# Feeding the experts of a mixture layer from a DRAM table instead of selection matmuls: 160 slots, a 32-row second tile in four column groups, four weight buffers

## The chip, the cores and the metric

One core of one Trainium2 chip runs the whole program. The metric is the device time in microseconds of one execution, as a median of several runs. One more execution was taken by the hardware profiler; all rows below come from that one.

## What is computed

One layer on 512 latent tokens of width 512 and a context of 8192 tokens, all in float32. In the reference:

```
x = x + cross_attention(layernorm(x), ctx)          # 16 heads, keys and values from 8192 context rows
x = x + self_attention(layernorm(x))                # softmax over a batch of one: value and output projections only
n = layernorm(x)
top_w, top_idx = top_k(n @ W_gate, 2); top_w = softmax(top_w)
for e in range(8):
    h = gelu(n @ W_in[e] + b_in[e])                 # 512 -> 2048
    y = h @ W_out[e] + b_out[e]                     # 2048 -> 512
    x = x + combine[:, e, None] * y                 # combine is zero for tokens that did not choose e
```

The reference computes every expert for every token; the kernel computes an expert only for the tokens that chose it (512 tokens, two choices, eight experts: 128 tokens an expert on average). With the seeded inputs the reference's gate gives the experts 113, 129, 159, 130, 134, 128, 92 and 139 tokens.

## The kernel before, in words

The change touches only the expert layer, the last 430 us of the span. Before it come the cross attention over the context, and `self_attention` (L770), in which SP already loads the first expert weights (`load_first`, L1025). `route` (L858) normalises x, computes the gate, the mask of the two choices, each token's rank within its expert (`r.rank`), the combine weights, and the flag `r.long`, which is set when an expert has more than SLOTS = 192 tokens.

`run_experts` (L1032) then walks over eight experts. Expert e has a column for each slot: 128 slots of a first tile, and 64 of a second tile that stand twice, so 256 columns. `select` (L1270) makes a 0/1 matrix of 512 tokens by 256 columns on VectorE; `gather` (L1149) multiplies the normalised tokens with it on TensorE, once for the high part and once for the low part, so that the tokens of the expert stand as columns. All large products are made of three fp32r products (high by high, high by low, low by high), which is why ScalarE rounds each weight tile to a high part (L1226, L1247) and VectorE subtracts to get the low part (L1267, L1306).

An expert is cut into four chunks (mc) of 512 hidden units. `hidden` (L1114) makes 4 x 3 x 4 = 48 matmuls of 256 columns for a chunk; ScalarE applies gelu; `output` (L1130) makes 12 fp32r matmuls of 512 columns for the first tile and, for the second tile, four plain fp32 matmuls in two column groups of 64 (L1144; each is two instructions in the trace, so 8). `turn_sel` (L1162) transposes the selection with 8 matmuls, and `scatter` (L1170) multiplies the expert's result (split again in high and low) with it, 16 matmuls of 512 columns an expert, which VectorE adds to x_sb (`add`, L1280).

The order on TensorE is written out by hand in `expert` (L1191): hidden 0, half of the scatter of the expert before, hidden 1, the other half, output 0, turn_sel, hidden 2, output 1, hidden 3, half of the gather for the next expert, output 2, the other half, output 3. Each engine has its own such list, and semaphores tie them. SP loads weights of 1 MB a transfer into two buffers of each kind, and waits for the low split or for `y_done` before it refills one. After the last expert four stores of 256 KB write x_sb to the output. A second call of `run_experts` (up to two more rounds of slots) stands behind the flag `r.long` and is skipped where no expert overflows.

Of the kernel before, what the change touches and what calls it, by code (L numbers as in the profile page):

```python
# [50 lines left out]
NX = 8  # L51
# [7 lines left out]
ROUNDS = -(-NQ // SLOTS)  # L59
# [710 lines left out]
def self_attention(nc, ctx, wv, bv, wo, bo, ident, x_sb, prefetch):  # L770
# [19 lines left out]

    with nc.Block() as block:
        @block.sync
        def _(sp):
            prefetch(sp)

# [62 lines left out]
def route(nc, ctx, w_gate, b_out, ident, x_sb, r):  # L858
# [6 lines left out]
    xn = sb("ro_xn", [P, QT, E])  # L865
# [16 lines left out]
    first = sb("ro_first", [P, QT, NX])  # L882
    second = sb("ro_second", [P, QT, NX])
# [12 lines left out]
    with nc.Block() as block:  # L896
# [6 lines left out]
        def _(pool):  # L903
# [3 lines left out]
            rounds = r.numbers[:, :].rearrange("p (r n) -> p r n", n=COLS)  # L907
            nc.gpsimd.iota(rounds[:, :, 0:P], pattern=[[SLOTS, ROUNDS], [1, P]], base=0, channel_multiplier=0,
                           allow_small_or_imprecise_dtypes=True).then_inc(made, 1)
            for copy in range(2):  # L910
                pool.wait_ge(made, copy + 1)
                nc.gpsimd.iota(rounds[:, :, P + copy * PAIRED:P + (copy + 1) * PAIRED], pattern=[[SLOTS, ROUNDS], [1, PAIRED]],
                               base=P, channel_multiplier=0, allow_small_or_imprecise_dtypes=True).then_inc(made, 1)
            pool.wait_ge(made, 3)
            nc.gpsimd.memset(every[:, :], 1.0).then_inc(made, 1)
            pool.wait_ge(made, 4)
            nc.gpsimd.affine_select(out=before[:, :], in_=every[:, :], compare_op=ALU.is_gt, fill=0.0,
                                    base=0, pattern=[[1, P]], channel_multiplier=-1).then_inc(made, 1)

        @block.tensor  # L920
        def _(pe):
# [8 lines left out]
            pe.wait_ge(made, 5)  # L930
# [25 lines left out]
        def _(dve):  # L956
# [29 lines left out]
            for t in range(QT):  # L986
                nc.vector.tensor_scalar(second[:, t, :], second[:, t, :], weight[:, 1, t:t + 1], None, ALU.mult).then_inc(link, 1)
            dve.wait_ge(masked, 1)
            dve.wait_ge(link, 5 + 5 * QT)
            for t in range(QT):  # L990
                nc.vector.scalar_tensor_tensor(r.combine[:, t, :], first[:, t, :], weight[:, 0, t:t + 1], second[:, t, :],
                                               ALU.mult, ALU.add).then_inc(link, 1)
# [6 lines left out]
            nc.vector.tensor_scalar(r.long[:, :], longest[:, :], float(SLOTS), None, ALU.is_gt).then_inc(done, 1)  # L999


class ExpertInputs:


    def __init__(self, nc, ctx):
        sb = lambda n, s: ctx.enter_context(nc.sbuf_tensor(n, s, F32))
        self.b_hidden = sb("ei_b_hidden", [P, NX, M // P])
        self.wi = [sb(f"ei_wi{b}", [P, ET, MC]) for b in range(2)]
        self.wo = [sb(f"ei_wo{b}", [P, MT, E]) for b in range(2)]

    def name_semaphores(self, nc, ctx, first_round):
        sem = lambda n: ctx.enter_context(nc.semaphore(f"ei{first_round}_{n}"))
        self.biases = sem("biases")
        self.wi_loaded = [sem(f"wi_loaded{b}") for b in range(2)]
        self.wo_loaded = [sem(f"wo_loaded{b}") for b in range(2)]

    def load_in(self, sp, w_in, e, mc):
        sp.dma_start(self.wi[mc % 2][:, :, :], w_in[bass.ds(e * E, E), mc * MC:(mc + 1) * MC]
                     .rearrange("(t p) m -> p t m", p=P)).then_inc(self.wi_loaded[mc % 2], 16)

    def load_out(self, sp, w_out, e, mc):
        sp.dma_start(self.wo[mc % 2][:, :, :], w_out[bass.ds(e * M + mc * MC, MC), :]
                     .rearrange("(t p) f -> p t f", p=P)).then_inc(self.wo_loaded[mc % 2], 16)

    def load_first(self, sp, w_in, b_in, w_out):  # L1025
        sp.dma_start(self.b_hidden[:, :, :], b_in).then_inc(self.biases, 16)
        for mc in range(2):
            self.load_in(sp, w_in, 0, mc)
            self.load_out(sp, w_out, 0, mc)


def run_experts(nc, ctx, rounds, w_in, b_in, w_out, ident, x_sb, out_dram, r, inputs):  # L1032
# [12 lines left out]
    expert_of = lambda step: step if STEPS == NX else step % NX  # L1045
# [6 lines left out]
    h = [sb(f"h{b}", [P, MT, COLS]) for b in range(2)]  # L1052
# [12 lines left out]
    bias_banks = [yp[:, t, :] for t in range(2)] + [hp[1][:, 2 * t:2 * t + 2, :].rearrange("p a n -> p (a n)") for t in range(2)]  # L1065
    move_g = move[:, :, :].rearrange("p a (b n) -> p (a b) n", n=COLS)
    b_ready, biased = map(sem, ("b_ready", "biased"))
# [7 lines left out]
    def guarded(eng, program):  # L1075

        if rounds[0] == 0:
            program()
        else:
            flag = eng.value_load(r.long[:, :], min_val=0, max_val=1)  # L1080
            with eng.If(flag > 0):
                program()

    with nc.Block() as block:
        @block.sync
        def _(sp):
# [11 lines left out]
            def program():  # L1098
                if rounds[0] > 0:
                    inputs.load_first(sp, w_in, b_in, w_out)  # L1100
# [4 lines left out]
                if rounds[0] > 0:  # L1105
                    sp.wait_ge(r.stored, 2 * 16 * QT)

            if rounds[0] > 0:
                sp.wait_ge(r.stored, 16 * QT)
# [3 lines left out]
        def _(pe):  # L1113
            def hidden(e, mc):  # L1114
# [4 lines left out]
                if rounds[0] == 0 and isinstance(n, int) and n == 1:  # L1119
                    pe.wait_ge(x_stands, QT)  # L1120
# [63 lines left out]
            def output_biases():  # L1184

                for t in range(QT):
                    last = nc.tensor.matmul(bias_banks[t], r.combine_t[:, t * P:(t + 1) * P], r.bo[:, :],  # L1187
                                            start=True, stop=True)
                last.then_inc(biased, 1)

# [20 lines left out]
            def program():  # L1211
                gather(0, 0)
                if rounds[0] == 0:
                    output_biases()
# [49 lines left out]
        def _(dve):  # L1264
# [5 lines left out]
            def select(e):  # L1270
                x = bass.ds(expert_of(e), 1)
                if STEPS == NX:
                    numbers = r.numbers[:, 0:COLS]
                else:
                    numbers = r.numbers[:, bass.ds((rounds[0] + e // NX) * COLS, COLS)]
# [177 lines left out]
```

## Time and profile before

| | |
|---|---|
| median of 3 runs | 1511.66 us (1506.25 to 1512.45) |
| span of the profiled execution, first to last instruction | 1510.6 us |
| start of the expert layer's first selection on VectorE | 1081.88 us |
| first hidden matmul | 1095.93 us |
| end of the last output matmul | 1494.9 us |
| expert layer's own stretch | 1081.9 to 1510.6 us |

The profile gives the span, not what lies around it; the span is 1.1 us under the median. A line of a group in the profile reads: line of the source, engine, operation, output tile, input tiles, shape, count; busy time in all and mean ns of one; idle time before them and who ended it. PE is the matrix engine, PEld its weight loads, DVE the VectorE, ACT the ScalarE, POOL the GpSimd. Matmuls overlap, so a mean duration is a latency; the spacing of matmuls is the length of a piece of the chain divided by its count.

### The profile page before, as it was taken

How to read it: one execution, taken by the hardware profiler on the slowest of the kernel's cores; microseconds unless marked ns; L12 is line 12 of the kernel's file. 1: busy time of each engine (PE TensorE's matmuls, PEld its weight loads, DVE VectorE, ACT ScalarE, POOL GpSimd, SP SyncE). 2: the span in 40 equal slices, each digit the busy share in tenths (PEclk: the TensorE clock that was granted, in tenths of full speed). 3: DMA queues.
4: the chain of work that ended last, by engine and by line, in shares of the span. 5: the costliest groups of instructions: out<-in, count | busy, mean ns of one | idle time of the engine just before them, and what ended most of it. 6: DMA issues, size and time to landing. Idle time of an engine off the chain costs nothing. (4 is left out here: it accounts for less than half of the span.)

```text
span 1510.6 us, 21218 instructions
## 1 busy us (share of the span) xinstructions
PE 1444.6 (96%) x7952; PEld 910.1 (60%) x7952; DVE 966.9 (64%) x846; ACT 811.0 (54%) x865; POOL 25.9 (2%) x24
## 2 busy tenths in 40 slices
PE   6999999999799999999999999977799999999996
PEld 4888888888433333333333333325688878887884
DVE  7444444443588888888888888865355556555653
ACT  4122122121488888888888888832264445444551
POOL 2000000000300000000000000000000000000000
PEclk9999999999899999999999999998599999999999
DMA  6855455454685555555555555203044544454441
GB/s 199 253 174 207 176 187 201 167 201 161 189 213 115 112 111 111 111 115 118 116 117 116 112 111 111 56 5 110 28 140 156 178 166 164 153 183 163 163 147 57
DMA packets 136180, 214.26 MB, mean 142 GB/s; under 512 B 7624, under 2 KB 40520, under 8 KB 136144
## 3 DMA queue, kind: packets, MB, share of 16 engines
q1 hardware_dynamic: 136144, 213.78, 48.9%
q8 instruction: 23, 0.38, 0.1%
q14 instruction: 13, 0.11, 0.0%
HBM read 159.23 MB, written 51.38 MB: 139 GB/s over the span
## 5 line engine op out<-in xcount | busy, mean ns | idle before, releaser
L659 ACT ACTIVATE at_p<-at_s 128x1024 f32<-128x1024 f32 x512 | 496.8, 1023 | 91.2 <-PE at_s L612 91.0
L679 DVE TENSOR_TENSOR p_sum<-p_sum,at_p 128x2048 f32 (+1 forms) x208 | 476.8, 2292 | 58.4 <-ACT at_p L659 50.9
L612 PEld LDWEIGHTS at_s<-q_stack,at_k 97*128 97x128 f32 x1024 | 172.8, 189 | 249.0 <-ACT at_p L659 162.2
L612 PE MATMUL at_s<-q_stack,at_k 97*128 (+1 forms) x1024 | 311.5, 424 | 7.7 <-PEq L440 7.0
L625 PE MATMUL at_o<-at_p,at_v 128*32 128x512 f32 x2048 | 273.0, 605 | 0.1
L409 ACT ACTIVATE sc_k_hi<-sc_kp,sc_bk 128x512 fp32r<-128x512 f32 x64 | 44.2, 691 | 125.8 <-PE sc_kp L377 125.8
L139 ACT ACTIVATE sc_c_hi<-sc_c 128x2048 fp32r<-128x2048 f32 x16 | 30.7, 1918 | 150.6 <-PE sc_vp L384 137.6
L1267 DVE TENSOR_TENSOR ex_wi_lo<-ei_wi,ex_wi_hi 128x2048 fp32r<-128x2048 f32 x32 | 73.3, 2289 | 51.2 <-ACT ex_wi_hi L1226 51.2
L341 DVE SCALAR_TENSOR_TENSOR sc_k_lo<-sc_kp,sc_bk,sc_k_hi 128x512 fp32r<-128x512 f32 x64 | 48.0, 750 | 89.3 <-ACT sc_k_hi L409 89.2
L349 DVE TENSOR_TENSOR sc_v<-sc_vp,sc_bv 128x512 f32<-128x512 f32 x64 | 44.1, 690 | 88.8 <-PE sc_vp L384 88.8
L1244 ACT ACTIVATE ex_h<-ex_hp,ex_b_cur 128x256 f32<-128x256 f32 x128 | 53.7, 471 | 86.7 <-PE ex_hp L1125 86.2
L625 PEld LDWEIGHTS at_o<-at_p,at_v 128*32 128x32 f32 x2048 | 40.3, 108 | 93.9 <-issue 92.9
L1306 DVE TENSOR_TENSOR ex_wo_lo<-ei_wo,ex_wo_hi 128x2048 fp32r<-128x2048 f32 x32 | 73.3, 2292 | 21.5 <-ACT ex_wo_hi L1247 21.5
L1125 PE MATMUL ex_hp<-ex_xg_hi,ex_wi_hi 128*128 128x256 f32 x512 | 85.3, 289 | 1.2 <-ACT ex_xg_lo L1231 1.2
L1125 PE MATMUL ex_hp<-ex_xg_hi,ex_wi_lo 128*128 128x256 f32 x512 | 82.9, 284 | 0.0
L1125 PE MATMUL ex_hp<-ex_xg_lo,ex_wi_hi 128*128 128x256 f32 x512 | 82.7, 284 | 0.0
L1125 PEld LDWEIGHTS ex_hp<-ex_xg_hi,ex_wi_hi 128*128 128x128 f32 x512 | 71.5, 193 | 14.2 <-issue 13.6
L377 PE MATMUL sc_kp<-sc_c_hi,sc_w_hi 128*128 128x512 f32 x256 | 70.1, 395 | 1.8 <-PEq L176 1.8
L1125 PEld LDWEIGHTS ex_hp<-ex_xg_hi,ex_wi_lo 128*128 128x128 f32 x512 | 71.3, 194 | 0.0
L1125 PEld LDWEIGHTS ex_hp<-ex_xg_lo,ex_wi_hi 128*128 128x128 f32 x512 | 71.0, 193 | 0.0
L377 PE MATMUL sc_kp<-sc_c_lo,sc_w_hi 128*128 128x512 f32 x256 | 70.1, 395 | 0.0
L377 PE MATMUL sc_kp<-sc_c_hi,sc_w_lo 128*128 128x512 f32 x256 | 70.1, 395 | 0.0
(202 smaller groups left out, 1657.6 us busy)
## 6 DMA issues: line engine op xcount, KB each, us to landing
at_k<-k_hi_scratch SPq DMA_DIRECT2D x128, 256.0 KB, 4.7
ei_wi<-w_in SPq DMA_DIRECT2D x32, 1024.0 KB, 7.3
ei_wo<-w_out SPq DMA_DIRECT2D x32, 1024.0 KB, 5.3
sc_c<-ctx_t SPq DMA_DIRECT2D x16, 1024.0 KB, 8.0
k_hi_scratch<-sc_k_hi SPq DMA_DIRECT2D x16, 1024.0 KB, 4.0
k_lo_scratch<-sc_k_lo SPq DMA_DIRECT2D x16, 1024.0 KB, 6.1
at_k<-k_lo_scratch SPq DMA_DIRECT2D x64, 256.0 KB, 4.3
at_v<-v_scratch SPq DMA_DIRECT2D x64, 256.0 KB, 5.0
```

What stands on the lines that cost most here:

```text
L341: nc.vector.scalar_tensor_tensor(k_lo[b][:, g, :], kp[g][:, :], bk[:, g:g + 1], k_hi[b][:, g, :].bitcast(F32), ALU.add, ALU.subtract).then ...
L349: nc.vector.tensor_tensor(v[b][:, t, :], vp[t][:, :], bv[:, :], ALU.add).then_inc(v_ready, 1)
L377: last = nc.tensor.matmul(kp[g][:, :], lhs[:, d, g * P:(g + 1) * P], rhs[b][:, d, :], start=(a == 0 and d == 0), stop=(a == 2 and d == ET ...
L409: nc.scalar.activation(k_hi[b][:, g, :], kp[g][:, :], ACT.Identity, bias=bk[:, g:g + 1]).then_inc(k_hi_ready, 1)
L612: last = nc.tensor.matmul(s[r][:, a * NQ:(a + 1) * NQ], k[c][:, j, t * P:(t + 1) * P], q_stack[:, bass.ds(it // PER_GROUP * (HG * NQ) + j ...
L625: last = nc.tensor.matmul(o[j * D:(j + 1) * D, :], v[c][:, t % KT, j * D:(j + 1) * D], p[r][:, j * NQ:(j + 1) * NQ], start=(t == 0), stop= ...
L659: nc.scalar.activation(p[t % PR][:, pair * 2 * NQ:(pair + 1) * 2 * NQ], s[u % SR][:, :], ACT.Exp, scale=SCALE).then_inc(p_ready[t % PR], 1)
L679: nc.vector.tensor_tensor(sums, sums, p[t % PR][:, :], ALU.add).then_inc(p_summed[t % PR], 1)
L1125: last = nc.tensor.matmul(hp[b][:, t, :], lhs[b][:, d, t * P:(t + 1) * P], rhs[:, d, :], start=(a == 0 and d == 0), stop=(a == 2 and d == ...
L1244: nc.scalar.activation(h[b][:, t, :], hp[b][:, t, :], ACT.Gelu, bias=b_cur[:, mc * MT + t:mc * MT + t + 1]).then_inc(h_ready, 1)
L1267: nc.vector.tensor_tensor(wi_lo[b][:, :, :], wi[b][:, :, :], wi_hi[b][:, :, :].bitcast(F32), ALU.subtract).then_inc(wi_lo_ready, 1)
L1306: nc.vector.tensor_tensor(wo_lo[b][:, :, :], wo[b][:, :, :], wo_hi[b][:, :, :].bitcast(F32), ALU.subtract).then_inc(wo_lo_ready, 1)
```

## The change

- The slots become CAP = 160 columns: 128 and a second tile of 32. The flag `r.long` now asks for more than 160 tokens. The rounds behind the flag start at slot 160.
- A DRAM table of 8 x 160 rows (521 floats each: the token, its number, its eight combine weights) is blanked by GpSimd during `self_attention`. After the routing, GpSimd sends each token's row to the rows of its two experts with 8 indirect DMAs of 128 rows. Expert 0 is still gathered by matmuls; for every later expert SP loads 160 rows from the table, TensorE transposes them (8 transposes), ScalarE and VectorE split them in high and low.
- x goes to a DRAM accumulator (four stores). Each expert's result is scaled with the combine weight on VectorE and added into the accumulator by two indirect DMAs with an add (128 rows and 32 rows). At the end one DRAM to DRAM copy of 1 MB writes the output. The selection for experts 1 to 7, its transposes and the scatter matmuls are gone.
- The second output tile is four fp32 matmuls, one for each 128 hidden rows of a chunk, each in a column group of 32; a matmul with a matrix `joins` adds the four groups once an expert (`join_parts`).
- Weights have four buffers of each kind, loaded a whole expert ahead.

The core of the diff:

```
+CAP = P + D
+ROUNDS = 1 + -(-(NQ - CAP) // SLOTS)
+ROWS = NX * CAP
+ROW = E + 1 + NX
+SPILL = ROWS + 2 * NQ
...
+        @block.gpsimd                       # in self_attention
+        def _(pool):
+            nc.gpsimd.memset(blank[:, :, :], 0.0).then_inc(blank_set, 1)
...
+            pool.dma_start(slots_dram[0:ROWS, :].rearrange("(t p) f -> p t f", p=P), blank[:, :, :]).then_inc(blanked, 16)
+            pool.wait_ge(blanked, 16)
...
-            nc.vector.tensor_scalar(r.long[:, :], longest[:, :], float(SLOTS), None, ALU.is_gt).then_inc(done, 1)
+            nc.vector.tensor_scalar(r.long[:, :], longest[:, :], float(CAP), None, ALU.is_gt).then_inc(done, 1)
...
+        self.wi = [sb(f"ei_wi{b}", [P, ET, MC]) for b in range(NMC)]
+        self.wo = [sb(f"ei_wo{b}", [P, MT, E]) for b in range(NMC)]
...
+def send_to_experts(nc, ctx, w_in, b_in, w_out, ident, x_sb, out_dram, r, inputs, slots_dram, acc_dram):
...
+        def _(sp):
+            def load_tokens(e):
+                sp.dma_start(tokens[:, :], slots_dram[bass.ds(e * CAP, P), 0:E]).then_inc(tokens_loaded, 16)
+                sp.dma_start(tail_tokens[:, :], slots_dram[bass.ds(e * CAP + P, D), 0:E]).then_inc(tokens_loaded, 16)
+            def expert(e, last):
...
+                    if mc == 1 and first:
+                        for t in range(QT):
+                            sp.wait_ge(x_stands, t + 1)
+                            sp.dma_start(acc_dram[t * P:(t + 1) * P, :], x_sb[:, t, :]).then_inc(x_stored, 16)
+                    if mc == 2 and first:
+                        sp.wait_ge(sent, 16 * 2 * QT)
+                    if mc == 2 and not last:
+                        wait_reuse(sp, turned, e)
+                        load_tokens(e + 1)
...
+            rolled(sp, NX, expert)
+            sp.wait_ge(landed, 2 * 16 * NX)
+            sp.dma_start(out_dram.rearrange("a t e -> (a t) e"), acc_dram[0:NQ, :]).then_inc(r.stored, 16)
...
+        def _(pool):
...
+            for t in range(QT):
+                for choice in range(2):
+                    nc.gpsimd.indirect_dma_start(
+                        out=slots_dram[:, :], out_offset=bass.IndirectOffsetOnAxis(ap=place_u[:, choice, t:t + 1], axis=0),
+                        in_=r.row[:, t, :], in_offset=None).then_inc(sent, 16)
+            pool.wait_ge(sent, 16 * 2 * QT)
+            for e in range(NX):
+                nc.gpsimd.dma_start(meta[:, :], slots_dram[e * CAP:e * CAP + P, E:ROW]).then_inc(meta_loaded, 16)
+                nc.gpsimd.dma_start(tail_meta[:, :], slots_dram[e * CAP + P:(e + 1) * CAP, E:ROW]).then_inc(meta_loaded, 16)
+                pool.wait_ge(meta_loaded, 32 * (e + 1))
...
+                for rows, which, ready in ((y, meta, y_ready), (tail_y, tail_meta, tail_y_ready)):
+                    pool.wait_ge(ready, e + 1)
+                    nc.gpsimd.indirect_dma_start(
+                        out=acc_dram[:, :], out_offset=bass.IndirectOffsetOnAxis(ap=which[:, 0:1].bitcast(U32), axis=0),
+                        in_=rows[:, :], in_offset=None, compute_op=ALU.add).then_inc(landed, 16)
+                pool.wait_ge(landed, 32 * (e + 1))
...
+            def turn_tokens(e):
+                pe.wait_ge(tokens_loaded, 32 * e)
+                for d in range(ET):
+                    nc.tensor.transpose(turn[:, d, 0:P], tokens[:, d * P:(d + 1) * P], ident[:, :])
+                    last = nc.tensor.transpose(turn[:, d, P:CAP], tail_tokens[:, d * P:(d + 1) * P], ident[0:D, 0:D])
+                last.then_inc(turned, 1)
+            def hidden(e, mc):
...
+                            last = nc.tensor.matmul(hp[b][:, t, 0:CAP], lhs[b][:, d, t * P:(t + 1) * P], rhs[:, d, :],
+                                                    start=(a == 0 and d == 0), stop=(a == 2 and d == ET - 1))
...
+            def output(e, mc):
...
+                for m in range(MT):
+                    last = nc.tensor.matmul(tp[m * D:(m + 1) * D, :], h[b][:, m, P:CAP], wo[mc][:, m, :],
+                                            start=(mc == 0), stop=(mc == NMC - 1))
+                last.then_inc(y_done, 1)
+            def join_parts(e):
+                pe.wait_ge(parts_ready, e + 1)
+                nc.tensor.matmul(tp[0:D, :], joins[:, :], parts[:, :], start=True, stop=True).then_inc(joined, 1)
+            def expert(e, last):
+                hidden(e, 0)
+                if not (isinstance(e, int) and e == 0):
+                    join_parts(e - 1)
+                hidden(e, 1)
+                output(e, 0)
+                hidden(e, 2)
+                output(e, 1)
+                hidden(e, 3)
+                if not last:
+                    turn_tokens(e + 1)
+                output(e, 2)
+                output(e, 3)
...
+        def _(dve):                          # end of an expert on VectorE
...
+                if not last:
+                    dve.wait_ge(xg_hi_ready, e + 2)
+                    nc.vector.tensor_tensor(xg_lo[:, :, :], turn[:, :, 0:CAP], xg_hi[:, :, :].bitcast(F32),
+                                            ALU.subtract).then_inc(xg_lo_ready, 1)
+                dve.wait_ge(y_done, NMC * (e + 1))
+                nc.vector.tensor_copy(parts[:, :], tp[:, :]).then_inc(parts_ready, 1)
+                dve.wait_ge(meta_loaded, 32 * (e + 1))
+                wait_reuse(dve, landed, 32 * e)
+                nc.vector.tensor_scalar(y[:, :], yp[:, :], meta[:, bass.ds(e + 1, 1)], None, ALU.mult).then_inc(y_ready, 1)
```

## Rows read from the trace of the kernel before

**Rows 1.** The page: busy shares, then granted clock and DMA share in 40 slices.

```profile
PE 1444.6 (96%) x7952; PEld 910.1 (60%) x7952; DVE 966.9 (64%) x846; ACT 811.0 (54%) x865; POOL 25.9 (2%) x24
...
PEclk9999999999899999999999999998599999999999
DMA  6855455454685555555555555203044544454441
```

**Rows 2.** Busy time by engine in stretches: prefetch, then one expert (last columns clock, DMA share, GB/s).

```profile
1017.00:1031.00 14.00, 6.61 (x23) 5.63 (x24) 12.39 (x24) 7.26 (x8) 0.00 (x0) 0.66 0.85 304
...
1202.00:1253.00 51.00, 51.00 (x332) 41.67 (x331) 29.10 (x36) 25.63 (x29) 0.00 (x0) 1.00 0.45 164
```

**Rows 3.** The chain that ended last, one expert: start us, length us, what.

```profile
1202.85 5.75 PE ex_hp L1125 x48
1208.61 1.84 PE ex_move L1180 x8
1210.44 2.72 PE ex_yp L1139 x12
1213.16 1.87 PE ex_yp L1144 x8
1215.03 1.05 PE ex_move L1166 x8
...
1226.44 5.95 PE ex_hp L1125 x48
1232.40 1.89 PE ex_move L1158 x16
...
1238.88 2.08 PE ex_move L1158 x16
```

**Rows 4.** Timeline of PE in the first hidden chunk, clock at half.

```profile
1096.93 1.05 PE L1125 MATMUL ex_hp<-ex_xg_hi,ex_wi_lo 128*128 128x256 f32 x4
1097.78 1.05 PE L1125 MATMUL ex_hp<-ex_xg_lo,ex_wi_hi 128*128 128x256 f32 x4
```

**Rows 5.** Groups by form, PE: the gate's 8-column matmuls, and four-group fp32 sums.

```profile
L633 PE MATMUL at_totals<-at_p,at_ones 128*32 128x512 f32 x384 | 50.0, 592 | 0.0
...
L927 PE MATMUL ro_gate<-ro_wg,ro_xt 128*128 128x8 f32 x32 | 7.0, 361 | 2.2 <-ACT ro_xt L948 2.2
```

**Rows 6.** Groups by form, PEld: weight loads of 128 and of 32 columns.

```profile
L1125 PEld LDWEIGHTS ex_hp<-ex_xg_hi,ex_wi_hi 128*128 128x128 f32 x512 | 71.5, 193 | 14.2 <-issue 13.6
...
L625 PEld LDWEIGHTS at_o<-at_p,at_v 128*32 128x32 f32 x2048 | 40.3, 108 | 93.9 <-issue 92.9
```

**Rows 7.** Timeline of the last expert's end: start us, length us, engine, line.

```profile
1485.67 1.92 ACT L1247 ACTIVATE ex_wo_hi<-ei_wo 128x2048 fp32r<-128x2048 f32 x1
...
1487.62 2.29 DVE L1306 TENSOR_TENSOR ex_wo_lo<-ei_wo,ex_wo_hi 128x2048 fp32r<-128x2048 f32 x1 [0.98 <-ACT ex_wo_hi L1247]
...
1489.97 0.50 PE L1139 MATMUL ex_yp<-ex_wo_hi,ex_h_hi 128*128 128x512 f32 x1 [0.45 <-DVE ex_wo_lo L1306]
...
1494.92 1.02 ACT L1254 ACTIVATE ex_y_hi<-ex_yp 128x1024 fp32r<-128x1024 f32 x1 [7.33 <-PE ex_yp L1144]
...
1503.18 1.41 DVE L1285 SCALAR_TENSOR_TENSOR x_sb<-ex_move,ff_combine,x_sb 128x512 f32<-128x512 f32 x2 [2.28 <-PE ex_move L1180]
```

**Rows 8.** Timeline of the layer's start.

```profile
1083.31 3.48 PE L1158 MATMUL ex_move<-ex_sel,ff_x_hi 128*128 128x256 f32 x16 [2.37 <-DVE ex_sel L1277]
...
1095.93 0.55 PE L1125 MATMUL ex_hp<-ex_xg_hi,ex_wi_hi 128*128 128x256 f32 x1 [1.21 <-ACT ex_xg_lo L1231]
```

**Rows 9.** DMA issues: KB each, median us from issue to landing.

```profile
ei_wi<-w_in SPq DMA_DIRECT2D x32, 1024.0 KB, 7.3
...
out<-x_sb SPq DMA_DIRECT2D x4, 256.0 KB, 2.0
...
sbo<-sb_out SPq DMA_DIRECT2D x1, 256.0 KB, 14.8
```

**Rows 10.** Groups by form, POOL: a long memset.

```profile
L575 POOL MEMSET p_sum<- 128x6144 f32 x1 | 5.2, 5237 | 0.1
```

More of the change, by code:

```diff
@@ L881, in route @@
     weight = sb("ro_weight", [P, 2, QT])
-    first = sb("ro_first", [P, QT, NX])
-    second = sb("ro_second", [P, QT, NX])
+    first, second = r.chosen[:, 0, :, :], r.chosen[:, 1, :, :]
+    weighted = sb("ro_weighted", [P, QT, NX])
     longest = sb("ro_longest", [1, 1])
@@ L914, in _ @@
-            pool.wait_ge(made, 3)
+                pool.wait_ge(made, copy + 2)
+                nc.gpsimd.iota(rounds[:, :, P + copy * PAIRED:P + (copy + 1) * PAIRED],
+                               pattern=[[SLOTS, ROUNDS - 1], [1, PAIRED]], base=CAP + P, channel_multiplier=0,
+                               allow_small_or_imprecise_dtypes=True).then_inc(made, 1)
+            pool.wait_ge(made, 4)
             nc.gpsimd.memset(every[:, :], 1.0).then_inc(made, 1)
-            pool.wait_ge(made, 4)
+            pool.wait_ge(made, 5)
@@ L920, in _ @@
+            pool.wait_ge(r.numbered, 2)
+            nc.gpsimd.iota(r.row[:, :, E:E + 1].bitcast(I32), pattern=[[P, QT], [0, 1]], base=0,
+                           channel_multiplier=1).then_inc(r.numbered, 1)
         @block.tensor
@@ L1075, in guarded @@
     def guarded(eng, program):
-        if rounds[0] == 0:
+        flag = eng.value_load(r.long[:, :], min_val=0, max_val=1)
+        with eng.If(flag > 0):
             program()
[L1079 to L1082, printed above, removed]
     with nc.Block() as block:
@@ L1098, in program @@
             def program():
-                if rounds[0] > 0:
-                    inputs.load_first(sp, w_in, b_in, w_out)
+                for t in range(QT):
+                    sp.dma_start(x_sb[:, t, :], out_view[:, t, :]).then_inc(reloaded, 16)
+                inputs.load_first(sp, w_in, b_in, w_out)
                 rolled(sp, STEPS, expert)
@@ L1182, in scatter @@
                 last.then_inc(scattered, 1)
[L1184 to L1189, printed above, removed]
             def expert(e, last):
@@ L1271, in select @@
                 x = bass.ds(expert_of(e), 1)
[L1272 to L1275, printed above, removed]
+                numbers = r.numbers[:, bass.ds(CAP + e // NX * COLS, COLS)]
                 for t in range(QT):
@@ L1320, in program @@
                 split_in(0, 0)
-                if rounds[0] == 0:
-                    dve.wait_ge(biased, 1)
-                    for t in range(QT):
-                        nc.vector.tensor_tensor(x_sb[:, t, :], x_sb[:, t, :], bias_banks[t], ALU.add).then_inc(x_stands, 1)
-                else:
-                    dve.wait_ge(r.stored, 16 * QT)
-                    dve.sem_inc(x_stands, QT)
+                dve.wait_ge(reloaded, 16 * QT)
+                dve.sem_inc(x_stands, QT)
                 rolled(dve, STEPS, expert)
```

286 lines of the change are left out of this document (242 added, 44 removed).

## The prediction

> **What bounds the kernel now.** I read the page first: PE is busy 96% of the span, DVE 64%, ACT 54%, POOL 2% [rows 1]. That is an average over stages, so I cut out one expert: in 51 us PE is busy all 51, DVE 29, ACT 26, at full clock, and DMA works at 0.45 of its time [rows 2]. The chain of waits says the same: through an expert it never leaves PE, and each piece starts where the one before ends [rows 3]. One expert is 50.5 us: four hidden chunks of 5.75 to 5.95 us (23.4), four times the first output tile at 2.73 (10.9), four times the second at 1.87 (7.5), two gather halves of 1.89 and 2.08 (4.0), the turned selection 1.05, and two scatter pieces of 1.84 (3.7). The sum is 50.5. So in this layer a microsecond taken from PE is a microsecond of the span, until ACT, DVE or a DMA ends last. The layer's loop runs from 1095.93 [rows 8] to about 1494.9 us, 399 us; the rest of the span is touched only at two edges.
>
> **The change part by part.**
>
> *Hidden matmuls, 256 to 160 columns.* There are 192 an expert, 1536 in all, and they are spaced 5.75/48 = 0.120 us. The first output tile has 512 columns at 2.73/12 = 0.2275 us. The line through both is 0.0129 + 0.00042 N, which gives 0.080 us at 160 columns: that is one end. But each matmul also loads 128 columns of weights, and no fp32r matmul under 256 columns is in the trace. Weight loads last 108 ns for 32 fp32 columns and 193 for the 128 fp32r columns here [rows 6]; the two give 85/96 = 0.89 ns a column, so 113 ns for 128. The cold rows say it more directly: at half clock four matmuls of 256 columns lie 1097.78 - 1096.93 = 0.85 us from the next four, 0.213 us each [rows 4], and the gate's matmuls with only 8 columns cost 7.0/32 = 0.219 us [rows 5] (plain fp32, so a neighbour and not the same thing). Under 256 columns the load sets the pace, not the columns. I take 0.115 us (113 plus the 2 ns I allow for the swap), between 0.080 and today's 0.120 as ends. If instead narrow fp32r matmuls fell to the fp32 rate, the price would be that of rival A. Gain: 1536 x 0.005 = 8 us, and 0 to 61 us by the ends.
>
> By the rows a load takes 193 ns from start to end and sets the pace at 8 columns. The Trainium skill, "TensorE: Matmul & The Clock Gate", section "LDWEIGHTS (loading the stationary operand)", gives a load as its columns divided by 1.2 ns, 107 ns here; by that the hidden part would gain 12 us more, an estimate from that page. [...]
>
> *Second output tile, two rounds of two groups to one round of four.* Today 8 instructions take 1.87 us a chunk [rows 3]. The attention stage has four groups of 32 columns: 384 instructions in 50.0 us, so 8 in 1.04 us [rows 5]; half of today's 1.87 is 0.94. I take 1.0, between them. Gain 0.87 x 32 = 28 us; ends 27 and 30.
>
> *Gather, selection transposes and scatter go.* 7 gathers of 3.97 (expert 0 keeps its own) are 27.8; 8 times 1.05 for the turned selection is 8.4; scatter in the loop for 7 experts 3.68 each is 25.8 (the last one lies behind 1494.9). Together 62.0 us.
>
> *What comes on PE.* Token transposes, 8 a turn, 7 turns: the 8 transposes of today take 1.05 us; half of them are narrower, I take 0.9, so 6.3; ends 3.7 and 7.4. `join_parts`: one fp32 matmul of 512 columns, two instructions; one round of the tile above without its neighbours, 0.9 us, 7 in the loop, 6.3 us; ends 0.86 and 1.04 each.
>
> *New stalls.* Output 3 needs the low split of its weights, which follows hidden 3, gelu, ACT's split of 1.92 and DVE's of 2.29. In the last expert today, where no gather fills the time, output 3 waits 0.45 us after output 2's 2.73 + 1.87 [rows 3, 7], so the helpers need 5.05 us from the end of hidden 3, with narrower gelus 4.9. In the new order PE has 0.9 + 2.73 + 1.0 = 4.6 us of work there: 0.3 us of stall for 7 experts, 1.2 for the last, against 0.45 today. Net 2.9 us. At the head of an expert, hidden 1 waits for a chain from the end of output 3: parts copy and scaling on DVE (two passes of 512 columns, 1.41 [rows 7]), bias and gap 0.4 as an estimate, ACT 1.92, DVE 2.29, about 6.0 us; PE has hidden 0 (5.5) and the join (0.9), 6.4. It holds with 0.4 us to spare; queued behind it are the h splits and the next wo split. ACT's 26 us [rows 2] lose three passes of 1.02 [rows 7] and some of each gelu, 22 are left; DVE loses the adds, the selection and one split and gets four passes of about 0.7, 27 are left of 29. In an expert of 39 neither binds on average. Where the cover fails, each 1 us costs 8.
>
> *DMA.* Weights stay 8.4 MB an expert but in 39 us: 215 GB/s, and some 10 more for tokens and results. The prefetch stretch moved 304 GB/s at share 0.85 [rows 2], so it fits, and each load is issued an expert ahead against 7.3 us to land [rows 9]. Four buffers are worth nothing by themselves: the chain of an expert shows no DMA [rows 3]. I cost them at 0; ends 0 and +10.
>
> *POOL's queue.* During self-attention POOL fills 5210 floats a partition: 5.2 us x 5210/6144 = 4.4 us [rows 10], then 2.7 MB go to DRAM beside 8.4 MB of weights: 11.1 MB at 304 GB/s are 37 us from 1017, so 1054 against the stage's end at 1052.5. Since both queues share, the table should be through before. Cost 0, ends 0 and +8. The 8 scatters of 128 rows are a kind of DMA that the trace lacks. Nearest rows: 256 KB land in 2.0 to 14.8 us [rows 9]. They start at about 1088 and must be done when SP reaches chunk 2 of expert 0, and the tokens must be there at the turn, about 1128: 40 us for 8, 5 us each. I take no stall; the upper end, 8 x 14.8 = 118 us in a row, would cost 80 once. Behind SP's wait on `sent` stand the token loads and the rest of expert 1's weights.
>
> *Start.* Both gathers now run without ACT between them, load-bound while cold, 0.213 x 32 = 6.8 us from 1083.3, then four bias matmuls, 3.4 to 4.2. DVE then needs four adds (2.8) and `joins` (0.3) before the loop may begin: 1083.3 + 6.8 + 3.8 + 3.1 = 1097, against 1095.93 today [rows 8]. Cost 1 us. While PE idles for those 3 us the clock stays low, and the first hidden chunk pays about 1.5 us more than today.
>
> *End.* Today 15.7 us lie behind the last output matmul (1494.9 to 1510.6): splits, two scatter rounds, adds that end at 1504.6, a store of 2.0 [rows 7, 9], and 3.7 to the end, the flag's part among them (1510.6 - 1504.6 less the store and its issue). New: parts 0.9, scaled y at 1.7, join, tail scaling until 3.2, two scatter-adds one behind the other on POOL, then 1 MB DRAM to DRAM, then 3.7 us of ending as today. Taking 4 us a scatter-add (between 2.0 and 14.8) and 7.3 for the copy: 3.2 + 5 + 7.3 + 3.7, about 19.5. Cost 4 us, ends -2 and +20. The Trainium skill, "DMA: Bandwidth & Descriptors", section "Anatomy of one DMA — SWDGE (gpsimd) path", puts a GpSimd DMA at 2.0 us plus bytes over 436 GB/s, 2.6 us here; no row has one, and by it the end would be about 2 us shorter.
>
> **The sum.** Gains 8 + 28 + 62 = 98; added 6.3 + 6.3 + 2.9 + 1.5 + 1 + 4 = 22; net 76. From 1510.6 that is a span of 1434.6, and with the 1.1 us of the median over the span 1436. An expert would take about 39.5 us.
>
> **Rivals.**
>
> A. *Narrow fp32r matmuls run at the fp32 rate* (slower). A round of fp32 matmuls of 512 columns is 0.94 us, 0.86 without its edges; in proportion 0.27 us at 160 columns. Against 0.115 that is 1536 x 0.155 = 238 us: 1674. It decides above 0.165 us a matmul, where 1536 x 0.05 eats the 76 us. For: nothing narrower than 256 is in the trace. Against: at half clock the 256-column rows run exactly one column a cycle, with no sign of an edge. 8%.
>
> B. *Helpers, weights or one-off transfers come late.* Slack at hidden 1 is 0.4 us and output 3 stalls already; 2 us more an expert and 10 us once give 1462. For: DVE goes from 57% to 69% of an expert and DMA from 0.45 to about 0.65. Against: the chain never leaves PE today. 13%.
>
> C. *Columns alone set the pace.* At 0.080 us hidden 0 plus join is 4.7 us, under the 6.0 us chain, so 1.3 us an expert comes back: 1436 - 54 + 10 = 1392. Against: the gate rows. 5%. [...]
>
> D. *POOL's chain sets the period* (slower). Two table reads and two scatter-adds in a row: at 14.8 us each 59 us an expert, DVE's scaling waits for the table read, and behind it the bias and the next splits: 1511 + 8 x 8.5 = 1579. It costs from 39.5 us a chain and loses from 50. 3%.
>
> E. *The change does not do what it says:* the busiest expert has 159 tokens of 160; two more in the kernel's own gate and 16 more expert steps of 50.5 us run, 2240. 2%.
>
> **How the numbers follow.** Main case 69%, with its own range 1420 to 1452. For 8 in 10 I reach into B and C: 1396 to 1476. About 0.5% (7.5 us) is what can be told from no change. Faster: 69 + 13 + 5 and a little of D, 87%. Same: 1%. Slower: A, the rest of D and E, 12%.
>
> **What would show it.** Hidden chunks of 48 matmuls in 5.5 us (3.8 for C, 13 for A); the second tile in 1.0 us; pieces of PE ending on each other with a wait near 0.3 us before output 3, on the low split of wo; an expert period of 39.5 us; no wait of PE for tokens; 19 us behind the last output matmul. Wrong it would be if the period is over 42 us, or if DVE waits for the table reads.

## The result and the profile after

The changed kernel took 1450.3 us (median of 4 runs, 1445.7 to 1451.2) against 1510.5 (4 runs, 1506.3 to 1512.5): 60 us less, ratio 0.9601, 95% interval 0.9577 to 0.9624. Forecast were 1436 and 76 us less. Its profiled run was the fastest of the four, 1445.7 us with a span of 1443.9, so from trace to trace [rows 1 to 10] 66.7 us of the span went: the layer's loop (from the first hidden matmul to the last output matmul) took 330.3 us instead of 399.0 (68.7 less), the part ahead of it 1.4 more, the part behind it 16.3 instead of 15.7.

Two lines of the page of the changed kernel, which answer to [rows 1]: PE still has 95%, and in the granted clock the half level covers a longer piece (slices 30 and 31).

```profile
PE 1370.8 (95%) x7608; PEld 847.3 (59%) x7608; DVE 950.6 (66%) x819; ACT 772.9 (54%) x841; POOL 73.6 (5%) x71
...
PEclk9999999999999999999999999999955999999998
```

The chain of waits through one warm expert of the changed kernel, against [rows 3] (start us, length us, what), and the busy time of that stretch, against [rows 2] (PE, PEld, DVE, ACT, POOL, then clock, DMA share, GB/s):

```profile
1354.46 5.52 PE se_hp L1203 x48
1359.98 2.77 PE se_yp L1217 x12
1362.76 0.99 PE se_tp L1221 x8
...
1378.55 0.12 PE se_turn L1187
1378.66 0.17 PE se_turn L1188
...
1380.14 2.96 PE se_yp L1217 x12
...
1384.10 2.95 PE se_yp L1217 x12
...
1393.56 0.98 PE se_tp L1228 x2
1394.54 1.50 PE se_hp L1203 x12
```

```profile
1354.00:1394.00 40.00, 40.00 (x284) 32.09 (x282) 26.18 (x29) 20.29 (x26) 4.19 (x4) 1.00 0.65 209
```

From one first chunk to the next it is 1394.54 - 1354.46 = 40.08 us, where it was 50.5. The chain is PE alone, as before: four hidden chunks of 5.52, the first output tile at 2.77 + 2.76 + 2.96 + 2.95, the second four times at 1.00, the turn of the tokens 1.60 (1378.55 to 1380.14), the join 0.98.

Expert 0 is the other half of the story. The chain at the layer's start, first of the changed kernel, then of the kernel before:

```profile
1094.51 2.48 DVE x_sb L1354 x4
1096.98 0.29 DVE se_joins L1355
...
1097.32 20.77 PE se_hp L1203 x96
1118.09 4.20 PE se_yp L1217 x12
```

```profile
1095.93 13.50 PE ex_hp L1125 x96
1109.44 2.75 PE ex_yp L1139 x12
```

The first two hidden chunks, 96 matmuls, take 20.77 us where two warm ones take 11.04, and the output behind them 4.20 instead of 2.77. The clock in these stretches (columns as above):

```profile
1097.00:1118.00 21.00, 20.68 (x97) 20.68 (x98) 9.20 (x11) 8.83 (x10) 1.14 (x2) 0.50 0.27 96
1118.00:1123.00 5.00, 5.00 (x21) 3.20 (x20) 3.08 (x4) 4.29 (x4) 0.00 (x0) 0.70 0.01 3
```

PE was busy for all of it, at the half level (1.2 GHz) until 3 us into the 512-column matmuls. Before the change the 256-column matmuls of the same place rose to the full level within 4 us.

The waits of PE from the loop's start on (us in total, times, longest; a third, of 0.8 us, is that of the last join for `se_parts`), and what hangs on POOL and the new transfers (busy us, mean ns; KB each, us to landing):

```profile
PE se_hp L1203 <- DVE se_joins L1355: 2.9, 1, 2.9
...
PE se_yp L1217 <- DVE se_wo_lo L1331: 1.2, 1, 1.2
```

```profile
L1160 POOL DMA_INDIRECT acc_scratch<-se_y,se_meta x8 | 13.3, 1666 | 246.0 <-DVE se_y L1342 246.0
L1160 POOL DMA_INDIRECT acc_scratch<-se_tail_y,se_tail_meta x8 | 10.9, 1366 | 28.3 <-DVE se_tail_y L1310 28.0 <-issue 0.3
L1147 POOL DMA_INDIRECT slots_scratch<-ff_row,se_place_u x8 | 7.9, 982 | 34.4 <-DVE se_place_u L1303 32.3 <-issue 2.1
```

```profile
se_tokens<-slots_scratch SPq DMA_DIRECT2D x7, 256.0 KB, 5.4
```

None of the transfers that the change brings is among the waits of PE: POOL spends 1 us on each of the eight scatters, the tokens land in 5.4 us, and POOL stands idle for DVE before its scatter-adds (246 us). DVE waited for a scatter-add once, 0.8 us.

### The profile page after: what moved, and what is told of

It reads as the page before. It is cut to its first block and busy times, and to the rows that moved or that the text cites. A ratio compares the mean times of both kernels' runs of the same rounds, so it can differ in the third digit from the quotient of the medians.

```text
span 1443.9 us, 20528 instructions
## 1 busy us (share of the span) xinstructions
PE 1370.8 (95%) x7608; PEld 847.3 (59%) x7608; DVE 950.6 (66%) x819; ACT 772.9 (54%) x841; POOL 73.6 (5%) x71
## 5 line engine op out<-in xcount | busy, mean ns | idle before, releaser
L1268 ACT ACTIVATE se_h<-se_hp,se_b_cur 128x160 f32<-128x160 f32 x128 | 43.4, 391 | 105.4 <-PE se_hp L1203 105.4
L1255 ACT ACTIVATE se_wi_hi<-ei_wi 128x2048 fp32r<-128x2048 f32 x32 | 61.2, 1913 | 69.4 <-DVE se_b_cur L1314 69.1
L1203 PEld LDWEIGHTS se_hp<-se_xg_hi,se_wi_hi 128*128 128x128 f32 x512 | 70.8, 200 | 29.6 <-issue 19.3
L1203 PE MATMUL se_hp<-se_xg_hi,se_wi_hi 128*128 128x160 f32 x512 | 83.6, 288 | 2.9 <-DVE se_joins L1355 2.9
L1331 DVE TENSOR_TENSOR se_wo_lo<-ei_wo,se_wo_hi 128x2048 fp32r<-128x2048 f32 x32 | 73.2, 2289 | 17.7 <-ACT se_wo_hi L1271 17.7
L1285 DVE TENSOR_TENSOR se_wi_lo<-ei_wi,se_wi_hi 128x2048 fp32r<-128x2048 f32 x32 | 73.2, 2286 | 17.6 <-ACT se_wi_hi L1255 17.6
L1203 PE MATMUL se_hp<-se_xg_lo,se_wi_hi 128*128 128x160 f32 x512 | 81.5, 284 | 0.0
L1203 PE MATMUL se_hp<-se_xg_hi,se_wi_lo 128*128 128x160 f32 x512 | 81.4, 284 | 0.0
L1203 PEld LDWEIGHTS se_hp<-se_xg_hi,se_wi_lo 128*128 128x128 f32 x512 | 71.0, 201 | 0.0
L1203 PEld LDWEIGHTS se_hp<-se_xg_lo,se_wi_hi 128*128 128x128 f32 x512 | 71.0, 201 | 0.0
```

The lines of the kernel that those rows point to most:

```text
L1203: last = nc.tensor.matmul(hp[b][:, t, 0:CAP], lhs[b][:, d, t * P:(t + 1) * P], rhs[:, d, :], start=(a == 0 and d == 0), stop=(a == 2 and d ...
L1255: nc.scalar.activation(wi_hi[mc % 2][:, :, :], wi[mc][:, :, :], ACT.Copy).then_inc(wi_hi_ready, 1)
L1285: nc.vector.tensor_tensor(wi_lo[mc % 2][:, :, :], wi[mc][:, :, :], wi_hi[mc % 2][:, :, :].bitcast(F32), ALU.subtract).then_inc(wi_lo_ready, 1)
L1331: nc.vector.tensor_tensor(wo_lo[b][:, :, :], wo[mc][:, :, :], wo_hi[b][:, :, :].bitcast(F32), ALU.subtract).then_inc(wo_lo_ready, 1)
```

## The experiments

Each is set beside the kernel before on the same chip. The changed kernel, run again among them, gave 1447.65 us (1447.2 to 1454.7) and 0.9595 (0.9573 to 0.9618); where a difference is small I also read the piece itself in the trace. Best for that is the stretch from the start of expert 0's gather to the end of the span: it was 363.7 us in both profiled runs of the changed kernel. What lies ahead of the gather differs from run to run (table below experiment 11).

**1. Bare matmuls of several widths.** Nothing but this, with a new weight tile for each:

```
for _ in range(110):   # 50 of 512 columns, then 60 of w, in the warm segments
    matmul(bank[:, 0:w], x_hi[:, i % 4, 128 columns], x_hi[:, (i + 1) % 4, 0:w])
```

> This kernel leaves out the whole layer: it copies the tokens to the output and beside that runs bare 128x128 fp32r matmuls, each with a weight load of its own, in segments. Eight segments start after some 16 us of rest on TensorE and run 110 matmuls of one width each, 64, 96, 128, 160, 192, 224, 256 and 512 columns; seven more run 50 matmuls of 512 columns first and then 60 of one width. Question one, what sets the spacing below 256 columns at the full clock. Theory 'the weight load sets it': 64 to 224 columns all stand 0.107 to 0.115 us apart, 256 at 0.115 to 0.120, 512 at 0.228. Rival 'the columns set it': 160 columns at 0.07 to 0.08 and in proportion, and the 0.112 of the changed kernel's first product comes from something else in it (a bank, an operand). Rival 'narrow fp32r is slow': 224 columns and fewer at 0.27 or more. Question two, whether the width decides if the clock rises. Theory 'narrow ones don't raise it': segments of 64 to 160 columns stay at the half clock for all their 110 matmuls (some 24 us), 256 and 512 columns leave it within about 15 us, 192 and 224 unsure. Rival 'width does not matter': every segment leaves the half clock after about the same time from its start.

Stretches inside segments, each row: length us, PE busy (count), granted clock, DMA. In order: 160 columns after rest; 192 after rest, its later part; 256 after rest, its first part; warm 64 at its end.

```profile
135.40:158.70 23.30, 23.30 (x109) 1.00 0.00 1
...
181.40:190.40 9.00, 9.00 (x82) 1.00 0.00 0
237.80:243.00 5.20, 5.20 (x24) 0.50 0.00 0
...
333.00:334.40 1.40, 1.40 (x9) 0.50 0.00 0
```

Spacing at the full level: 64, 96, 128, 160, 192 and 224 columns all 0.112 us, 256 0.120, 512 0.227. At the half level 64 to 256 columns are all 0.213. So under 256 columns the columns do not set the pace. What these rows hold constant is the load of 128 x 128 weights, and the trace of the kernel before has a row that speaks for the load and against a fixed price of an instruction: eight plain fp32 matmuls whose weight tile has one column.

```profile
L391 PE MATMUL sc_kp<-head_rows,sc_product 128*1 128x4 f32 x8 | 0.3, 166 | 1.0 <-DVE sc_product L361 1.0
```

They start 0.025 us apart, at the full level.

The granted clock of the first row of the stretches can't be right: the record reads 1.00 from the start of this program, while 23.30/109 is 0.213 us and a weight load takes 333 ns, exactly as at 237.8, where the record says 0.50; at the full level a load takes 192 ns. Read by the spacing: after the rest, 64, 96, 128 and 160 columns stayed at the half level for all 110 matmuls; 192 and 224 left it after about 30, 256 after 24, 512 after 11. Behind 50 matmuls of 512 columns, which end at the full level, 64 and 96 columns fell to half after 47 and 44 of them, and 128 and more kept the full level for all 60.

**2. Longer.** The same with 240 of each width.

> Bare 128x128 fp32r matmuls again, the whole layer left out (the tokens are copied to the output): segments of 240 matmuls after some 16 us of rest with 160, 176 and 192 columns, and 50 matmuls of 512 columns followed by 240 of 128, 144 and 160 columns. Theory 'below some width between 160 and 192 the half clock is kept, at the full clock 160 hold it': the cold 160 stay 0.213 us apart for all 240 (51 us), 192 rise after about 30, 176 on either side; the warm 160 stay at 0.112 for all 240, while the warm 128, which held for 60, fall back to 0.213 before the end if the level that holds it lies just above them. Rival 'it is only a matter of time': the cold 160 rise too, somewhere after the 110 already seen.

Stretches of 160 and 176 columns after rest, 192 after it rose, and warm 160:

```profile
16.80:67.60 50.80, 50.80 (x239) 1.00 0.00 1
84.20:135.00 50.80, 50.80 (x239) 1.00 0.00 1
...
156.00:179.80 23.80, 23.80 (x216) 1.00 0.00 1
...
320.00:348.30 28.30, 28.30 (x248) 1.00 0.01 1
```

160 and 176 columns stayed 0.213 us apart for 51 us without a pause (the clock column is again wrong in these two rows); 192 rose after 17. Warm 128, 144 and 160 kept 0.112 for all 240, so my guess that 128 would fall was wrong. In these rows a stretch of 160-column matmuls keeps whichever level it starts at. That is what the changed kernel showed: half in expert 0's first product, full from there on.

**3. Expert 0's hidden matmuls at 256 columns.**

```diff
-matmul(hp[b][:, t, 0:CAP], lhs[...], rhs[:, d, :])
+cols = 256 if e == 0 else CAP          # columns 160 to 255 of xg_hi, xg_lo are zero
+matmul(hp[b][:, t, 0:cols], lhs[...], rhs[:, d, 0:cols])
```

> Expert 0's matmuls of the first product run over 256 columns instead of 160 (96 zero columns more), the other seven experts as they are. Theory 'the narrow first product keeps the clock at half': in expert 0 the clock rises within the first 96 matmuls, as it did before the change; that chunk takes 13 to 14 us instead of 20.8 and the first output chunk 2.8 instead of 4.2, so the kernel is 8 to 9.5 us faster than the changed kernel, about 1441 us. Rival 'the 2.9 us gap ahead of it, or the chip's own phase, keeps it low': 96 matmuls at the half clock take 21 to 23 us, and the time is 0 to 1.5 us longer.

1442.7 us (1440.8 to 1448.1), ratio 0.9549 (0.9533 to 0.9564), the interval clear of the changed kernel's. The chain of this kernel (its gather started at 1090.4 us, 10 us later than in the changed kernel's profile):

```profile
1107.50 13.53 PE se_hp L1209 x96
1121.03 2.75 PE se_yp L1223 x12
```

20.77 + 4.20 became 13.53 + 2.75, 8.7 us, by making each matmul do more; from the gather's start to the end it is 7.8 us less. The gap of 2.9 us ahead of it was still there. So the theory that the narrow first product keeps the clock at half holds.

**4. The gap alone.** The joining matrix made ahead of the four adds to the tokens.

```diff
 place_rows()
+nc.vector.tensor_reduce(joins, ...)
 dve.wait_ge(lo_gathered, 1)
 ...
 for t in range(QT): tensor_tensor(x_sb[:, t, :], x_sb[:, t, :], bias_banks[t], add)
-nc.vector.tensor_reduce(joins, ...)
```

> The matrix that joins the four column groups is made ahead of the four adds of the biases to the tokens instead of behind them; TensorE waited 2.9 us for it before expert 0's first product. Theory 'the narrow first product keeps the clock at half': the wait goes, the chunk still takes 20 to 21 us: 2.0 to 3.0 us faster than the changed kernel. Rival 'the gap keeps it low': without the gap the clock rises early in the chunk, and 9 us more go: 10 to 12 us faster. Rival 'the next wait is the same': another operand is as late, 0 to 0.5 us.

1446.2 us (1445.6 to 1448.4), ratio 0.9577 (0.9562 to 0.9592). The chain:

```profile
1095.94 3.41 PE se_hp L1180 x4
1099.35 20.70 PE se_hp L1203 x96
1120.05 4.59 PE se_yp L1217 x12
```

The gap went and the clock did not rise any sooner, so the rival that the gap holds the clock down is out. The gap was 2.9 us; from the gather's start to the end 2.2 are left of them (output 0 alone took 0.4 longer). By the medians it is 1.5 to 4, and the interval overlaps that of the changed kernel.

**5. All experts at 224 columns.** As in 3, with 224 and without the condition.

> All eight experts' matmuls of the first product run over 224 columns instead of 160 (64 zero columns more). Theory 'below some 224 columns the weight load sets the pace': 40% more columns cost nothing, a product of 48 stays at 5.52 us and an expert at 40.1 us, and expert 0's first one falls from 20.8 to 13 to 14 us as the clock rises in it: 8 to 9.5 us faster than the changed kernel, about 1442 us. Rival 'the columns count': 224 columns at 0.157 us by the ratio of the columns would be 7.5 us a product and 60 us more in all. A rise of the clock as in the bare matmuls (after 30 of 224 columns) is what the width theory adds.

1442.4 us (1438.9 to 1443.1), ratio 0.9539 (0.9522 to 0.9557). Expert 0, and a warm chunk:

```profile
1102.15 12.94 PE se_hp L1212 x96
...
1303.84 5.55 PE se_hp L1212 x48
```

40% more columns in all 1536 matmuls cost 0.03 us in 5.52, and expert 0 won 9.3; from the gather's start to the end it is 8.1 us less. This shows both readings inside the kernel: at 160 columns the columns do not set the pace, and with wider matmuls the clock rises in expert 0.

**6. The turn grouped.**

```diff
 for d in range(ET):
     transpose(turn[:, d, 0:P], tokens[...])
+for d in range(ET):
     last = transpose(turn[:, d, P:CAP], tail_tokens[...])
```

> The token turn's eight transposes run as four of 128 rows and then four of 32 rows, instead of by turns. Theory 'going between a full and a narrow tile costs': the turn falls from 1.60 us to 0.9 to 1.1, in seven experts, 3.5 to 5 us faster than the changed kernel. Rival 'each of the eight has its own price': 1.5 to 1.6 us still, 0 to 0.5 us faster.

1446.2 us (1442.1 to 1447.3), ratio 0.9566 (0.9548 to 0.9585). The turn fell to 0.90 us (1182.30 to 1183.20), so going to and fro between the 128-row and the 32-row form was 0.7 of the 1.60. Grouped, the 32-row transposes are 0.062 us apart, so a weight tile of 32 rows goes below the floor of 0.112. But the expert fell only from 40.08 to 39.57, because a wait came up behind it (its waits, and the chain ahead of output 3):

```profile
PE se_yp L1218 <- DVE se_wo_lo L1332: 2.8, 8, 1.2
```

```profile
1340.81 0.68 ACT se_h L1269 x2
1341.48 1.82 ACT se_wo_hi L1272
...
1343.32 2.30 DVE se_wo_lo L1332
...
1345.75 3.01 PE se_yp L1218 x12
```

That is the stall the forecast had placed there (0.3 us for 7 experts, 1.2 for the last); the slow turn had covered it. 3.5 to 5 us were expected of this edit; from the gather's start to the end it is 2.8, and the interval of the medians overlaps that of the changed kernel.

**7. Grouped turn, and the fourth chunk's split of wo ahead of its activations.**

```diff
 wait_reuse(act, y_done, n - 1)
+if mc == NMC - 1: wo_hi split (ACT), and wo_lo on DVE ahead of its h splits
 for t in range(MT): gelu ...
-wo_hi split
+if mc < NMC - 1: wo_hi split
```

> The token turn is grouped as in the earlier run, and for the fourth chunk of each expert the second weight's split (ScalarE's rounding copy, VectorE's subtraction) runs before that chunk's activations instead of behind them. Theory 'the split chain was next in line behind the turn': the waits of TensorE on the split's low part (2.8 us with the grouped turn alone, 1.2 us in the last expert of the changed kernel) go, an expert takes 39.3 to 39.4 us instead of 40.08 (39.57 with the grouped turn alone), and the time is 5.5 to 6.5 us under the changed kernel, about 1442 us. Rival 'the activations' own chain is as long': TensorE waits for the low part of the hidden tile instead, and 0 to 1 us is gained on the grouped turn alone (1446 to 1444 us).

1443.2 us (1440.6 to 1444.5), ratio 0.9556 (0.9537 to 0.9575). The wait is gone from all eight experts, an expert takes 39.3 us, and from the gather's start to the end it is 6.7 us less. PE in one of them, busy throughout:

```profile
1304.00:1343.30 39.30, 39.30 (x287) 31.78 (x283) 26.11 (x29) 20.47 (x25) 4.25 (x4) 1.00 0.68 230
```

**8. Two weight buffers instead of four,** loaded in the order of before: `load_in(e + (mc + 2) // 4, (mc + 2) % 4)`.

> Two weight buffers for each of the two weights instead of four, loads issued in the order of before the change. Theory 'four weight buffers are worth nothing, the loads have slack': 0 to 0.5 us to the changed kernel, no wait of TensorE or ScalarE on a weight longer than 0.3 us. Rival 'with two the loads come late': each chunk of 10 us needs two loads of 1 MB, and a load that starts only when its buffer's last reader is done lands late by 1 to 2 us in each of 32 chunks: 30 to 60 us slower.

1450.2 us (1447.1 to 1455.7), ratio 0.9605 (0.9578 to 0.9632): no difference that can be told, and in the trace 0.2 us from the gather's start to the end. I was wrong in one thing. ScalarE did wait for weights, 1.4 us in each of seven experts, where with four buffers it did not:

```profile
ACT se_wi_hi L1255 <- DMA ei_wi<-w_in: 9.5, 7, 1.7
```

It never reached PE, whose waits were the same as in the changed kernel. Four buffers are worth nothing here.

**9. The second tile in one column group.**

```diff
-matmul(tp[m * D:(m + 1) * D, :], h[b][:, m, P:CAP], wo[mc][:, m, :], start=(mc == 0), ...)
+matmul(tp[0:D, :], h[b][:, m, P:CAP], wo[mc][:, m, :], start=(mc == 0 and m == 0), ...)
```

> The second output tile's four matmuls of a chunk go into one column group instead of four beside each other; the joining matmul stays, with zeros in the three groups left. Theory 'the four groups run beside each other and that is the gain': 1.00 us becomes 3.4 to 3.6 us (eight passes at 0.43), in 32 chunks 77 to 83 us slower than the changed kernel, so slower than before the change. Rival 'most of the 1.00 us is not the columns': 1.0 to 2.0 us a chunk, 0 to 32 us slower.

1530.5 us (1526.8 to 1531.8), ratio 1.0123 (1.0101 to 1.0145), slower than before the change. One chunk's second tile:

```profile
1304.09 3.55 PE se_tp L1222 x8
```

2.55 us more in each of 32 chunks are 82 us; the medians are 83 apart, the stretch from the gather's start to the end 81. The four groups do run beside each other, and without them the change would have lost 1.2%.

**10. The gains together:** expert 0 at 224 columns, joining matrix early, and experiment 7.

> All together: expert 0's first product over 224 columns, the joining matrix made ahead of the adds, the turn grouped, the fourth chunk's split ahead of its activations. If the gains add: 8 (clock) + 3 (gap) + 6 (turn and split) = 17 us under the changed kernel, 1430 to 1434 us. Rival 'the gap's rest time and the clock hang together': without the gap the clock rises at another place in expert 0's first product, and the sum is off by up to 4 us either way.

1428.9 us (1428.1 to 1431.8), ratio 0.9468 (0.9449 to 0.9486), 19 us under the changed kernel on the chip that ran it again; by the trace 17.8 from the gather's start to the end. 17 were expected.

**11. And the gather at 256 columns,** `sel` and its matmuls `0:256` instead of `0:CAP`.

> The version with all four edits, and the gather's 32 matmuls ahead of expert 0 also over 256 columns instead of 160. Theory 'width decides, and what is ahead of the first product counts': the clock rises within the second half of the gather, as it did before the change in its 256-column gather, and stands or comes back sooner in expert 0's first product, which takes 11 to 12.5 us instead of 13.7; with the gather's end and the bias matmuls 2 to 6 us faster, 1423 to 1427 us. Rival 'the bias matmuls let it fall again': the gather's rise is lost before the first product, which stays at 13 to 14 us, and 0 to 2 us are gained (1427 to 1429 us).

1426.7 us (1423.9 to 1431.7), ratio 0.9455 (0.9430 to 0.9480). The chain of its profiled run, the fastest of the five:

```profile
1082.62 3.43 PE se_turn L1179 x16
1086.04 1.86 PE se_hp L1179 x16
1087.91 1.05 PE se_yp L1186 x2
...
1091.53 7.98 PE se_hp L1213 x48
```

The second half of the gather and the bias matmuls now run at the full level (1.86 us for 16, and 1.05 where it was 2.00). From the gather's start to output 0 it is 21.8 us, with experiment 10 28.0. The first product fell back to half for part of its way, and the wo split became the next thing late. The medians are 2.2 us apart and their intervals overlap, so beyond the profiled run, where it is 6.4 us from the gather's start to the end, this gain isn't shown. It is the fastest version of all, by that much.

The profiled runs side by side (us; the medians are of all runs of each kernel, the other columns of the profiled one):

| | median | gather starts | from there to the end |
|---|---|---|---|
| before | 1510.5 | 1083.3 | 427.3 |
| changed | 1450.3 | 1080.2 | 363.7 |
| changed, again | 1447.7 | 1081.7 | 363.7 |
| 3, expert 0 at 256 columns | 1442.7 | 1090.4 | 355.9 |
| 4, gap alone | 1446.2 | 1085.1 | 361.5 |
| 5, all at 224 columns | 1442.4 | 1085.1 | 355.5 |
| 6, turn grouped | 1446.2 | 1084.4 | 360.9 |
| 7, and split moved | 1443.2 | 1084.4 | 357.0 |
| 8, two buffers | 1450.2 | 1084.2 | 363.9 |
| 9, one column group | 1530.5 | 1084.9 | 445.1 |
| 10, gains together | 1428.9 | 1080.5 | 345.9 |
| 11, and the gather | 1426.7 | 1082.6 | 339.4 |

The start of the gather moves by up to 10 us although no experiment changed what stands ahead of the expert layer. The last column is the same in both runs of the changed kernel, and from the gather's start to the loop it is 17.1 us in all eight rows whose code there is the same (changed twice, 3, 5, 6, 7, 8, 9).

## Why the prediction was right, and where it was not

The mechanism held: PE is the bound, and what leaves PE leaves the span. The loop's 68.7 us come out of the pieces, by the forecast's terms:

- *Hidden matmuls:* 0.115 us by the chunk (5.52/48), as taken, while neighbours inside a chunk are 0.112 apart; a chunk of before was 5.75 to 5.95, so an expert gained 1.3 us, 10.6 in all where 8 stood. That the columns do not set the pace is shown (experiments 1, 5), and with it the columns' line of rival C is refuted; that the load does is argued, with the one-column row for it. The 0.213 us at half clock, in which rival A also read one column a cycle, is the same from 64 to 256 columns and says nothing of the columns.
- *Second tile:* 1.00 as taken, 28 us. *Gather, selection turn, scatter:* 62 us, all gone.
- *First output tile:* taken as unchanged, it rose from 10.9 to 11.4 an expert, 4 us in all. The two that follow narrow forms (the turn's 32 rows, the tail's 32 columns) are 0.2 longer. With one column group it was 2.94 as well, so the four groups are not the reason; what is stays open.
- *Turn:* 1.60 instead of 0.9, 5 us in all. The step that failed priced eight transposes by a row whose eight all have one form. *Join:* 0.98 against 0.9.
- *Stalls:* 0.3 before output 3 did not come, since the long turn covered it (experiment 6 brings it out); 1.2 in the last expert came. 2 us better than forecast.
- *Cold start:* the big miss. I took 1.5 us more than before; it was (20.77 - 11.04) + (4.20 - 2.77) = 11.2 against 13.50 - 11.5 = 2.0, so 9.2 more. The step that failed is "while PE idles for those 3 us the clock stays low": it laid the loss to the gap, and supposed that the narrower matmuls would then rise as those of 256 columns had. Experiment 4 took the gap away and won 2 to 3 us with the clock as low as before, experiments 3 and 5 gave the width back and won 8 to 9.
- *Start:* 1.4 against 1 looks right and is luck. The gather began 3.1 us sooner than in the profiled run of before, 2.3 of them already there at the end of the attention (the first add to x_sb behind it starts at 1003.7 against 1006.0), which the change doesn't touch. From the gather's start to the loop it is 17.1 us, where it was 12.6 and the forecast's terms give 13.7. The step that failed is the price of the bias matmuls, 3.8 us beside a gather at half clock. They took 4.2 before and 7.1 now (the kernel before, then the changed one):

```profile
1086.79 1.91 PE ex_yp L1187 x4
1088.70 2.31 PE ex_hp L1187 x4
```

```profile
1087.35 2.00 PE se_yp L1180 x2
1089.35 1.71 PE se_tp L1180 x2
1091.06 3.43 PE se_hp L1180 x4
```

  The granted clock was 0.84 from 1087 to 1091 us before and is 0.50 from 1087 to 1094 now: the 256-column gather had brought it up, the 160-column one does not. With 256 columns given back to the gather (experiment 11) they take 3.6. So the width cost 3 us here on top of the 9 in expert 0.
- *End:* 16.3 against 19.5 (the terms as written add to 19.2). The copy was issued 7.7 us behind the last output matmul where 3.2 + 5 stood, and landed in 5.2 where 7.3 stood; POOL spent 1.66 and 1.36 us on the two scatter-adds.
- *POOL and DMA* at 0: right, as the waits and experiment 8 show.

The balance of the loop: 10.6 + 28 + 62 - 4 - 11.2 - 6.9 - 0.8 - 9.2 = 68.5, against 68.7 in the trace. From trace to trace the forecast was 9 us too good. The clock (8 in the loop, 3 ahead of it), the turn (5) and the output tile (4) were missed; the hidden chunks, the stalls and the end gave back 8, and the earlier gather another 3. The other 7 us of the distance between the medians and 76 lie in the profiled pair: before was profiled at 1512.45, above its median, and after at 1445.7, below. The table puts such differences ahead of the gather. They go with the granted clock: among the runs of before, those with a mean of 0.979 have spans of 1504.1 to 1508.1 us, those with 0.974 and 0.975 have 1509.8 to 1511.8. By estimate 0.004 of 1510 us is 12 us more at half the clock, worth 6 where PE is the bound. Why the clock differs from run to run is open.

The Trainium skill, "TensorE: Matmul & The Clock Gate", section "LDWEIGHTS (loading the stationary operand)", gives 107 ns for 128 columns; the measured pace under 256 columns, 112 ns, agrees but for 5 ns. The formula N/2.4 + 2.5 ns in its section "Back-to-back issue gap", which that section gives for an isolated matmul and calls too low at small N, makes 69 ns of 160 columns; no run here met it.

## What to carry to other kernels

A matmul with a weight tile of its own has a floor, here 0.112 us for a tile of 128 x 128 in fp32r: columns below 256 save next to nothing, so before cutting them ask what the cut does in the stretches at the half clock, and try zero columns there. Before a small gain is read from two times, find a stretch that repeats from run to run, as the one from the gather's start does here. Read the forms in a sequence, not only its count: eight transposes cost 1.60 us by turns and 0.90 grouped. And when a piece on the path gets shorter, look for the stall it was covering; here the stall took back 0.2 of the 0.7 us an expert, until the split was moved too.

## What was not expected of the hardware

The half level stood through 51 us of unbroken 160-column matmuls, and the full level through 240 of the same; PE was as busy there as in the 192-column stretch beside it, which rose. The recorded granted clock read 1.00 at the start of a program that ran at half; spacing (0.213 against 0.112 us) and the weight load's length (333 against 192 ns) told the truth.
